# Expert blocks of two 64-slot units in the column halves of TensorE, in a two-layer gated cross-attention and mixture-of-experts kernel

## The reference

```python
# layer 0: quantized cross-attention of 16 heads, then experts; layer 1: attention of 8 heads, then experts
x = x + tanh(g_xattn[l]) * attention_l(norm(x), ctx)
x = x + tanh(g_ffn[l]) * experts_l(norm(x))
# experts_l, for each token: the 8 (layer 0) or 6 (layer 1) best of 32 experts by a sigmoid router,
# weighted to a sum of 2.5 or 1, and a shared expert that sees every token
y = sum(w[e] * (silu(h @ Wg[e].T) * (h @ Wu[e].T)) @ Wd[e].T for e in chosen) + shared(h)
```

## Time and profile before

| | us |
|---|---|
| median of 3 runs | 890.02 |
| lowest and highest | 890.01, 892.17 |
| span of the profiled execution | 931.3 |
| busy: PE, DVE, ACT, POOL | 741.2, 535.8, 437.5, 480.9 |

### The profile page before, as it was taken

The page is one execution under the profiler, slowest core; times in us unless marked ns, Lnnn a source line. Parts: engine busy times, 40 slices in busy tenths (PEclk is TensorE's granted clock), DMA queues, the critical chain, the costliest instruction groups (busy, mean ns, idle before and its releaser), DMA issues.

```text
span 931.3 us, 20204 instructions
## 1 busy us (share of the span) xinstructions
PE 741.2 (80%) x5678; PEld 544.3 (58%) x5719; DVE 535.8 (58%) x1323; ACT 437.5 (47%) x1058; POOL 480.9 (52%) x530
## 2 busy tenths in 40 slices
PE   6657777767687878999999999548856579999974
PEld 4535455544455665677777777425545467777753
DVE  5989879789784533344344444277653444444435
ACT  3568776666663112444444444236633015555540
POOL 3817665787886551333433433375246535555550
PEclk9869875775857798999999999857877789999997
DMA  8909999999999945656666666378026435555538
GB/s 281 371 10 184 172 164 193 177 216 216 202 187 248 331 159 174 189 182 198 197 188 199 191 187 198 138 281 299 16 77 176 152 114 180 167 171 172 159 108 313
DMA packets 222085, 175.53 MB, mean 188 GB/s; under 512 B 146698, under 2 KB 200922, under 8 KB 220954
## 3 DMA queue, kind: packets, MB, share of 16 engines
q1 hardware_dynamic: 207978, 132.52, 56.2%
q0 software_dynamic: 13728, 41.17, 12.3%
q10 hardware_dynamic: 272, 0.52, 0.1%
HBM read 87.92 MB, written 52.69 MB: 151 GB/s over the span
## 4 chain that ended last, share of the span: by engine, by line
PE 42%; issue 11%; POOL 11%; DVE 11%; DMA 10%; ACT 3%; SPq 3%; another core or an unknown queue 2%; POOLq 0%; DVEq 0%; ACTq 0%
PE psum L982 15%; PE psum L1015 11%; DMA pT<-p 6%; POOL p L1710 3%; POOL xs_dram L1723 3%; PE psum L994 3%; DVE nmax L1321 3%; PE psum L948 3%; POOL y_dram L1733 3%; PE psum L970 2%; DMA W<-y_dram 2%; PE psum L841 2%; ACT e L1169 1%; SPq L765 1%
## 5 line engine op out<-in xcount | busy, mean ns | idle before, releaser
L1733 POOL DMA_INDIRECT y_dram<-ybuf,idxi x174 | 167.4, 962 | 232.7 <-ACT ybuf L1218 186.7
L1500 DVE COPY hT<-psum 88x256 f32<-88x256 f32 (+2 forms) x214 | 74.2, 347 | 214.6 <-PE psum L994 103.0
L982 PE MATMUL psum<-W,xTs 128*128 x696 | 196.0, 405 | 0.7 <-issue 0.7
L1169 ACT ACTIVATE e<-psum,nmax 128x1024 f32<-128x1024 f32 x128 | 142.4, 1115 | 57.6 <-DVE nmax L1321 40.6
L1710 POOL TENSOR_SCALAR p<-e 128x1024 f16<-128x1024 f32 x128 | 133.9, 1046 | 65.6 <-ACT e L1169 38.9
L1321 DVE TENSOR_REDUCE nmax<-psum 128x1 f32<-128x1024 f32 x128 | 152.3, 1219 | 20.5 <-PE psum L841 17.3
L1723 POOL DMA_INDIRECT xs_dram<-xaug,posi x112 | 110.3, 985 | 69.2 <-issue 31.9
L1208 ACT ACTIVATE sg<-psum 128x176 f32<-128x176 f32 (+2 forms) x214 | 61.1, 286 | 161.9 <-PE psum L982 82.4
L1218 ACT ACTIVATE ybuf<-psum,dot 128x256 f32<-128x256 f32 x174 | 82.6, 474 | 110.3 <-PE psum L1015 100.9
L982 PEld LDWEIGHTS psum<-W,xTs 128*128 128x128 f32 x696 | 115.9, 193 | 23.2 <-issue 2.9
L841 PE MATMUL psum<-kstack,qstack 128*128 128x512 bf16 x215 | 93.2, 511 | 40.4 <-ACT e L1169 33.2
(11 more groups left out here) (223 smaller groups left out, 1140.9 us busy)
## 6 DMA issues: line engine op xcount, KB each, us to landing
xs<-xs_dram SPq DMA_DIRECT2D x174, 160.0 KB
W<-in_wffn SPq DMA_DIRECT2D x15, 1024.0 KB, 14.8
xs_dram<-zeros SPq DMA_DIRECT2D x2, 5120.0 KB, 25.6
oT<-in_wffn SPq DMA_DIRECT2D x96, 88.0 KB
osb_v<-in_wffn SPq DMA_DIRECT2D x94, 88.0 KB
W<-y_dram SPq DMA_DIRECT2D x6, 1024.0 KB, 6.7
W<-y_dram SPq DMA_DIRECT2D x8, 768.0 KB, 9.2
W<-in_wffn SPq DMA_DIRECT2D x4, 768.0 KB
```

The source lines that it names most:

```text
L982: last = pe.matmul(out, xTs[:, n % 2, k, :], Wv[layer][:, k, :, :, bass.DynSlice(of_block[q][0], 1), :], start=k == 0, stop=k == KD - 1)
L1169: act.activation(e[:, s % E_RING, :], bank(s_bank(s), 2), ACT.Exp, bias=nmax[:, s % S_RING:s % S_RING + 1], accum_out=esum[:, t, head:head ...
L1733: pool.indirect_dma_start(y_dram[layer][:, :], bass.IndirectOffsetOnAxis(idxi[:, slot:slot + 1], 0), ybuf[:, b % Y_RING, :], None).then_in ...
```

## The change

A block has two units of 64 slots now, each with an expert of its own. There are ceil(159 / 2) = 80 blocks in layer 0 and 64 in layer 1. The first unit takes the left half of TensorE's columns and the first 64 rows of the output, the second the right half. The first unit's weights are read as before. For the second, VectorE copies the gate and up weights of its expert into one of two buffers `gu2` (in the place of `xT`), two blocks ahead, and in layer 1 its down weights into one of three buffers `dn2`; VectorE reads the second expert's numbers in lists of four. In layer 0 a block loads the down weights of both experts, in four slots in place of eight: SP those of the first unit, four blocks behind its x loads, ScalarE those of the second, behind `y_block_out`; ScalarE issues the first four blocks' share before its unit 22. SP loads x in two pieces of 64 rows and reads three lists in place of two in layer 0, two in place of one in layer 1. The tables have two columns for the two units. Half as many rows of the DRAM tables are zeroed at the start.

```diff
+SUB, HALF = (2, 2), P // 2
+SR = tuple(P // n for n in SUB)
+BLOCKS = tuple(-(-((T * k + EXPERTS * (r - 1)) // r) // n) for k, r, n in zip(TOP, SR, SUB))
+XS_RING, DN_RING, DN2_RING, Y_RING, Y2_RING, IDX, IDX_RING = 8, 4, 3, 4, 4, 4, 16
...
+        def down_in(queue, b, j, expert):
+            slot = b % DN_RING
+            rows = wffn[0][SHARED[0]:, :, 2 * D:].rearrange("j (e c s) n -> j e c s n", e=EXPERTS, s=2)
+            for half in range(2):
+                queue.dma_start(dn[slot][half * TILES[0]:(half + 1) * TILES[0], j, :, :],
+                                rows[:, bass.DynSlice(expert, 1), :, half, :].rearrange("j e c n -> j (e c) n")
+                                ).then_inc(dn_in[slot], 16)
...
+                    n = SR[layer]
+                    for j in range(SUB[layer]):
+                        sp.dma_start(xs[j * n:(j + 1) * n, slot, :],
+                                     xs_dram[layer][bass.DynSlice(rows[j], n), :]).then_inc(xs_in[slot], 16)
+
+                def first_down_in(b, expert):
+                    if b >= DN_RING:
+                        sp.wait_ge(cf["down"], unit_of_block(b - DN_RING) + 1)
+                    down_in(sp, b, 0, expert)
...
                     for b in range(BLOCKS[layer]):
                         if b and b % IDX == 0:
-                            table = table_of(layer, b)
-                        block_in(layer, b, *table[b % IDX])
+                            earlier = experts
+                            rows, experts = table_of(layer, b)
+                        block_in(layer, b, [r[b % IDX] for r in rows])
+                        if layer == 0 and b >= IDX:
+                            first_down_in(b - IDX, earlier[b % IDX])
...
+                        pe.wait_ge(cf["gu2"], n + 1)
                         for k in range(KD):
-                            last = pe.matmul(out, xTs[:, n % 2, k, :],
-                                             Wv[layer][:, k, :, :, bass.DynSlice(of_block[q][0], 1), :],
-                                             start=k == 0, stop=k == KD - 1)
+                            pe.matmul(out[0:HALF, :], xTs[:, n % 2, k, 0:HALF],
+                                      Wv[layer][:, k, :, :, bass.DynSlice(of_block[q][0], 1), :],
+                                      start=k == 0, stop=k == KD - 1, skip_group_check=True)
+                            last = pe.matmul(out[HALF:P, :], xTs[:, n % 2, k, HALF:P], gu2[layer][n % 2][:, k, :],
+                                             start=k == 0, stop=k == KD - 1, skip_group_check=True)
...
+                        pe.matmul(out[0:HALF, :], hT[0:rows, q % 2, at:at + HALF], first, start=c == 0, stop=c == parts - 1,
+                                  skip_group_check=True)
+                        last = pe.matmul(out[HALF:P, :], hT[0:rows, q % 2, at + HALF:at + P], second, start=c == 0,
+                                         stop=c == parts - 1, skip_group_check=True)
...
                     if first <= q - 2 < end and routed(q - 2):
                         y_block_out(q - 2)
+                        b = units[q - 2][2]
+                        if layer == 0 and b + DN_RING < BLOCKS[0]:
+                            later_down_in(b + DN_RING)
+
+                def later_down_in(b):
+                    if b == 0:
+                        act.wait_ge(cp["tab"], 1)
+                        act.wait_ge(cp["y_ps"], NT)
+                    _, experts = nc.values_load_multi_w_load_instructions(
+                        tab[0:1, 1, 1, b:b + 1], engines=(mybir.EngineType.Activation,), min_val=0, max_val=EXPERTS - 1)
+                    down_in(act, b, 1, experts[0])
...
+                    if i == FIRST_DOWN:
+                        for b in range(DN_RING):
+                            later_down_in(b)
                     ffn(0, i)
...
+                    dve.tensor_copy(gu2[layer][n % 2].rearrange("p k (g j r) -> p (k g) j r", g=2, r=ROWS),
+                                    Wkg[layer][:, :, :, bass.DynSlice(expert, 1), :].rearrange("p c j e r -> p c j (e r)")
+                                    ).then_inc(cf["gu2"], 1)
...
+                    if q + 2 < end and routed(q + 2):
+                        second_gate_up(q + 2)
+                    if layer == 1 and q < end and routed(q):
+                        second_down(q)
```

More of the change, by code:

```diff
@@ L739, in table_of, with block_in @@
                 def table_of(layer, b):
[L741 to L743 removed]
+                    at = slice(b, min(b + IDX, BLOCKS[layer]))
+                    rows = [nc.values_load_multi_w_load_instructions(
+                        tab[0:1, 0, j, at], engines=(mybir.EngineType.SP,), min_val=0, max_val=EXPERTS * SEG - SR[layer])[1]
+                        for j in range(SUB[layer])]
                     if layer == 1:
[L745 to L750, removed]
+                        return rows, None
+                    return rows, nc.values_load_multi_w_load_instructions(
+                        tab[0:1, 1, 0, at], engines=(mybir.EngineType.SP,), min_val=0, max_val=EXPERTS - 1)[1]
+                def block_in(layer, b, rows):
                     slot = b % XS_RING
@@ L758, in block_in @@
                         sp.wait_ge(cf["idx"], done_before(layer, b, XS_RING))
[L759 to L767, removed]
+                    n = SR[layer]
+                    for j in range(SUB[layer]):
[5 more added lines that the diff above has]
+                    down_in(sp, b, 0, expert)
                 def blocks_in(layer):
                     sp.wait_ge(cp["tab"], layer + 1)
-                    table = table_of(layer, 0)
+                    rows, experts = table_of(layer, 0)
                     sp.wait_ge(scattered[layer], 16 * NT * TOP[layer])
@@ L932, in spread @@
                     for i in range(4):
-                        last = pe.matmul(bank(7)[:, i * P:i * P + nb], rep[:, i, :], ident[:, 0:nb], start=True, stop=True)
+                        pe.matmul(bank(7)[:, i * nb:(i + 1) * nb], rep[:, i, :], ident[:, 0:nb], start=True, stop=True)
+                    for j in range(1, SUB[layer]):
+                        at = j * SR[layer]
+                        last = pe.matmul(bank(7)[0:1, (3 + j) * nb:(4 + j) * nb], rep[:, 3, at:at + 1], ident[:, 0:nb],
+                                         start=True, stop=True)
                     last.then_inc(cp["rep_ps"], 1)
@@ L1447, in tables @@
[L1447 to L1452, removed]
@@ L1453, in tables @@
-                        dve.scalar_tensor_tensor(junk[:, 2, :], expert_no[:, :], expert, count[:, :], ALU.is_equal, ALU.mult,
-                                                 accum_out=own_count)
+                        before_it, own_count, nth, latest, rows, start, inside = [bv[:, i, 0:n] for i in range(7)]
+                        expert, lower, upper, row = [bv[:, i, 0:n] for i in range(8, 12)]
+                        no = unit_no[:, layer, 0:n]
+                        for j in range(n):
+                            dve.scalar_tensor_tensor(junk[:, 3 * j, :], endb[:, :], no[:, j:j + 1], nblk[:, :], ALU.is_le,
+                                                     ALU.mult, accum_out=before_it[:, j:j + 1])
+                            last = dve.scalar_tensor_tensor(junk[:, 3 * j + 1, :], endb[:, :], no[:, j:j + 1],
+                                                            ones[:, 0:EXPERTS], ALU.is_le, ALU.mult,
+                                                            accum_out=expert[:, j:j + 1])
@@ L1455, in tables @@
+                        step(last)
+                        for j in range(n):
+                            dve.scalar_tensor_tensor(junk[:, 3 * j + 2, :], expert_no[:, :], expert[:, j:j + 1], count[:, :],
+                                                     ALU.is_equal, ALU.mult, accum_out=own_count[:, j:j + 1])
                         dve.tensor_scalar(inside, expert, EXPERTS - 1.0, float(SEG), ALU.min, ALU.mult)
-                        step(dve.tensor_scalar(nth, before_it, row_no[:, :], -1.0, ALU.subtract, ALU.mult))
```

117 lines of the change are left out of this document (85 added, 32 removed).

## The result

The changed kernel takes 979.02 us (median of 4 runs, 969.86 to 984.62) against 890.33: a ratio of 1.094, interval 1.087 to 1.102. The forecast was 903, its range ended at 926. Slower was right; the size was wrong by a factor of seven (89 us in place of 12.6). The ratio leaves out the run of 984.62, which was in a slower state.

What follows compares the result with a forecast made beforehand. TensorE was taken to set both expert stages, with SP next at 93% used; after the change SP would set layer 0. Terms 4.6 + 1.5 + 6 + 0.5 = +12.6 us took 890.0 to 903, range 866 to 926.

Steps and rivals of the forecast that it cites:

- SP's work: Layer 0's blocks: SP's loads and lists take 12.5 us per four blocks, longer than TensorE's; body +6 us.
- Layer 1: Layer 1's blocks: three engines nearly level, 2.15 us a block, 138 us against 79 x 1.74 = 137; +0.5 us.
- The carried time: Whole kernel: priced stages carry over unchanged from the 931.3 us trace to the 890.0 us runs; 944 and 903.
- ScalarE's first batch: Before layer 0's blocks: four reads and eight loads take 7 us, delaying unit 22's silu and the last scatter; +4.6 us.
- Two column halves: TensorE in both layers' blocks: halves run at once, four mode switches at 0.12 us each; 2.97 and 2.03 us a block.
- the rival "faster": Both layers: switches half hidden, SP's reads fit idle time, TensorE sets 2.73 and 1.9 us a block; 863 us, chance 0.20.
- VectorE's copies: Both layers' blocks: weight copies of 0.53 us (704 numbers) and 0.36 (384), hidden in layer 0, about TensorE's block in layer 1.
- The rival of a shared path: Layer 1: VectorE's copies wait for POOL's scatter, 2.83 us a block, +44 us, together 946; chance 0.07.
- The tables: Routing tables of both layers: extra small instructions, a dependent step and a matmul per layer; +1.5 us in all (0 to 3).

Runs made afterwards that it cites:

- SP's checks out: The changed kernel with only the range checks behind the numbers SP reads from the tables left out; 912.43 us, ratio 1.027 against the kernel before.
- the two traces of before: The unchanged kernel before: its first trace spans 931.3 us; traced once more, it spans 894.0 and ran in 895.75 us.
- down in halves: The kernel before with layer 0's down matmul as two column halves using the same weights, 95 blocks of one expert; 917.61 us, ratio 1.031.

## Why the prediction was wrong, by its steps

*SP's work* is the step that failed. That "SP becomes what layer 0 waits for" was right; the size of the term was not, nor the wait by which it acts. 2.13 us a block and 12.5 per four were 2.45 and 14.5, and +6 for layer 0's body was +53. A load of 64 rows issues no faster than one of 128, and not as fast: 0.66 us to the next issue against 0.56; I had allowed only a lower end for what no row showed. The weights of a block took 1.10 to 1.14 us where I had 1.01, the lists up to 4.8 where I had 4.3, and the sum took 12.5 out of its own 12.7. From the x load of block 8 (375.65) to that of block 79 (634.24), 17 groups of four and three blocks, SP is 40 us later than by 12.5 a group; 3 more stand ahead of that and 5 behind it, where SP waits for the down matmuls of earlier blocks. Nor did the down matmul wait for weights, as I had it: that was 3.3 us. X came late, and it holds up VectorE, whose program order passes it on to blocks that have all they need. The trace of before had that wait already, 25.4 us of it, hidden behind TensorE's work; the prediction took x as being there.

*Layer 1* was +0.5 and is +25. I took "79 x 1.74 = 137" from a trace with stalls of its own; undisturbed it is 79 x 1.53 = 121, so that 64 x 2.0 alone is +7 (+8 with SP's checks out). The other 17 are SP again. I had counted three engines within 0.2 us "in order of each other" and took 2.15, but SP's four blocks, put at 7.5 us, took 8.3 to 8.7 (x loads of every fourth block start at 798.7, 807.0, 815.5, 824.2 and 832.5), and TensorE's take 8.0. Every fourth block stalled and took 3.1 us, and then came the clock: from 835.4 to 862.7 it is 0.50, and seven blocks take 3.53 where 2.00 is normal; with the block in which it fell that is 12 us.

*The carried time.* "931.3 becomes 944, and 890.0 becomes 903" took the 41 us for time outside the stages priced. Between the two traces of before 37 us differ: 4.4 at the start, 17.3 in layer 1's attention, and 16.6 in layer 1's blocks; these were a stage that was priced, by the 1.74 of the slow trace.

*ScalarE's first batch* cost 6.7 us in place of 4.6. It kept ScalarE for 7.84 us between two silus where I had 7 (6.4 to 7.4). In the earlier trace rows unit 22 came late by itself, after 1.86 us of idle time where 1.13 is usual, and I took that off; and the forecast's own two ends, 342.40 and 347.3, are 4.9 apart, not 4.6. Behind that batch, ScalarE's loads cost nothing, as forecast: with SP's checks out TensorE is busy for 197.3 of 198 us beside them.

*Two column halves*: right. They run together, and a change of mode was 0.14 us in layer 0 (0.12 taken, 0.2 the end), 3.07 a block against 2.97; the rival "faster", with half of it hidden and 2.73 a block, fell by that. The Trainium skill says, in TensorEngine Tiling (Array Packing), Key Properties, that a change of tiling mode drains the engine; the down matmul in halves agrees, with 0.284 us for two changes. By SP's term alone this didn't matter in layer 0, as the forecast said.

*VectorE's copies*: right, 0.50 us (704 numbers) and 0.35 (384). The rival of a shared path fell: of the copies of layer 0, those beside a scatter (17 of 80, over 0.25 us in common) took 0.53 in the median and 0.77 at most, the others 0.50, and the scatters beside a copy took 0.96 in the median like the others, so they don't exclude each other for a scatter's 0.95. The section SBUF: two separate sides of the Trainium skill (SBUF — State Buffer), read as that rival read it, is not borne out by these copies.

*The tables* (+1.5): layer 0's start is 8.2 late, 6.7 of it the batch. The other 1.5 were there already at the silu of unit 21, whose start differs by 7 us between two executions that do the same work up to there, so a cost of the tables is neither shown nor excluded.

## What to carry to other kernels

An issuing queue that is 93% used is the next bound: taking work off it changed nothing here (0.997), putting work on it cost 160 us. Price each new issue, list and check on it, with an upper end for every shape that the trace doesn't show. Before pricing a stage, hold the traced span against the timed runs, and find the stage that differs. A wait that stands in an engine's program order ahead of present work turns one late load into a stall of all.

## What the runs showed of the hardware

- The issue of a load of 64 rows took SP 0.48 us, of 128 rows 0.36 (medians in layer 0 of the changed kernel and of before, rows of 1280 bytes in both).
- A range check behind a number read into a register cost 0.25 us on SP; a list of four takes 1.35 us in the median with them (layer 0, changed) and 0.34 without (SP's checks out).
- A change between full width and column halves cost 0.14 us on TensorE (27.0 us for 95 blocks of two changes, down in halves).
- After stalls of 1.1 to 1.5 us in every fourth block of layer 1, TensorE ran at the 1.2 GHz level for 27 us (835.4 to 862.7), in which the profile has it busy throughout; with SP's checks out the same stage is at 2.4 GHz from 760 to 870 us.
- Two executions of the kernel before differed by 37 us of span, 34 of them in layer 1.
